# The delta rule's mixer: shifted sums from TensorE to ScalarE and VectorE, TensorE left with the turns

## The reference

```python
def fractal_mixer(x, conv_w):
    out = 2.0 * x
    for i in range(conv_w.shape[0]):            # 4 taps
        dil = 2 ** i                            # back by 1, 2, 4, 8 tokens
        x_shift = jnp.pad(x, ((0, 0), (dil, 0), (0, 0)))[:, :l, :]
        out = out + x_shift * conv_w[i, :, 0] + x * conv_w[i, :, 1]
    return out

frac = rmsnorm(fractal_mixer(x, frac_conv_w), mixer_norm_w)
gate = sigmoid(x @ frac_gate_w + frac_gate_b)
return core + gate * frac                       # core: the delta rule itself
```

## Time and profile before

| | before |
|---|---|
| median of 3 runs | 2610.37 us (2606.3 to 2613.95) |
| the profiled execution: time, span | 2605.69 us, 2603.9 us |
| PE busy | 2413.8 us (93%) |
| DVE busy | 1696.0 us (65%) |
| ACT busy | 1216.3 us (47%) |
| POOL busy | 1334.0 us (51%) |
| mean granted TensorE clock | 0.976 of full speed |

### The profile page before, as it was taken

How to read it: one execution, slowest core, us unless ns; L and a number is a source line. 1 busy time by engine, 2 the same in 40 slices (tenths; PEclk the granted TensorE clock), 3 DMA queues, 4 the chain that set the end, 5 groups by cost and what they waited for, 6 DMA issues and landing times. The chain is left out here.

```text
span 2603.9 us, 56605 instructions
## 1 busy us (share of the span) xinstructions
PE 2413.8 (93%) x20854; PEld 2007.2 (77%) x20854; DVE 1696.0 (65%) x4060; ACT 1216.3 (47%) x3095; POOL 1334.0 (51%) x1465
## 2 busy tenths in 40 slices
PE   4899999999999999878999999988899999999998
PEld 3788888888888888756777877756677778778776
DVE  4576777767677767576767767326756746747664
ACT  2656666666666666455444445114333333332332
POOL 3676776767676767256555555214522323322322
PEclk8999999999999999989999999988999999999999
DMA  4000100000000000012112111206112112212211
GB/s 141 7 10 9 45 17 11 9 10 10 10 10 9 9 5 5 15 31 45 42 47 49 36 53 43 55 31 187 33 52 68 62 42 74 66 42 62 64 39 58
DMA packets 156688, 105.05 MB, mean 40 GB/s; under 512 B 85168, under 2 KB 134832, under 8 KB 156416
## 3 DMA queue, kind: packets, MB, share of 16 engines
q1 hardware_dynamic: 131072, 62.83, 8.9%
q10 hardware_dynamic: 25344, 38.60, 4.8%
HBM read 80.51 MB, written 20.88 MB: 39 GB/s over the span
## 5 line engine op out<-in xcount | busy, mean ns | idle before, releaser
L920 POOL TENSOR_TENSOR a_bm<-a_bias,a_mask_add 128x512 f32<-128x512 f32 (+3 forms) x512 | 437.8, 871 | 191.0 <-DVE a_nm L674 186.0
L1529 POOL TENSOR_TENSOR m_hid_part<-m_hid,m_hid_part 128x512 fp32r<-128x512 f32 x176 | 239.5, 1361 | 564.1 <-ACT m_hid_part L1438 561.0
L830 ACT ACTIVATE a_S<-a_S,a_nm 128x512 f32<-128x512 f32 (+3 forms) x512 | 289.2, 565 | 346.4 <-DVE a_nm L674 343.6
L674 DVE CUSTOM_DVE_ANT_0 a_S<-a_S,a_bm,a_nsn 128x512 f32<-128x512 f32 (+3 forms) x512 | 275.4, 545 | 141.2 <-PE a_S L438 136.9
L461 PE MATMUL a_O<-a_v,a_PT 128*128 128x64 f32 x2560 | 342.4, 265 | 0.0
L461 PEld LDWEIGHTS a_O<-a_v,a_PT 128*128 128x128 f32 x2560 | 328.4, 193 | 0.0
L1450 ACT ACTIVATE m_hid<-m_G 128x512 f32<-128x512 f32 x176 | 105.4, 599 | 408.4 <-PE m_G L1384 371.3
L438 PE MATMUL a_S<-a_kT,a_qT 128*128 128x384 f32 (+3 forms) x1024 | 284.3, 359 | 3.5 <-DVE a_nm L674 3.0
L1401 PE MATMUL m_Y<-m_hid_part,m_down_high 128*128 128x512 f32 x704 | 257.3, 406 | 11.9 <-POOL m_hid_part L1529 11.1
L1611 DVE TENSOR_TENSOR m_hid<-m_hid,m_U 128x512 f32<-128x512 f32 x176 | 121.0, 687 | 223.6 <-PE m_U L1384 189.7
L1384 PE MATMUL m_G<-m_in,m_gate_high 128*128 128x512 f32 x704 | 251.5, 398 | 1.6 <-POOL m_up_low L1523 1.6
(11 more groups left out here) (314 smaller groups left out, 5240.2 us busy)
## 6 DMA issues: line engine op xcount, KB each, us to landing
m_spread<-s_w ACTq DMA_DIRECT2D x64, 256.0 KB, 3.3
m_spread<-s_w ACTq DMA_DIRECT2D x128, 128.0 KB, 2.9
a_x<-in_x SPq DMA_DIRECT2D x32, 128.0 KB, 2.1
s_hT<-a_hT SPq DMA_DIRECT2D x32, 128.0 KB, 2.1
d_x<-in_x SPq DMA_DIRECT2D x8, 512.0 KB, 4.8
d_h<-s_hT SPq DMA_DIRECT2D x8, 512.0 KB, 5.4
s_xg<-d_xg SPq DMA_DIRECT2D x8, 512.0 KB, 3.1
d_x<-s_xg SPq DMA_DIRECT2D x8, 512.0 KB, 4.5
```

What stands on the lines that cost most here:

```text
L674: dve.tensor_tensor_reduce(S[:, n % S_SLOTS, 0:w], SB[n % 2][:, 0:w], bm[:, n % BM_SLOTS, 0:w], -1.0, nsn[:, tile % 2, h:h + 1], ALU.add, ...
L830: act.activation(S[:, n % S_SLOTS, 0:w], S[:, n % S_SLOTS, 0:w], ACT.Exp, scale=-1.0, bias=nm[:, tile % 2, h:h + 1], accum_out=den[:, tile ...
L920: pool.tensor_tensor(bm[:, n % BM_SLOTS, 0:w], bias[:, h, L - w:L], mask_add[b % 2][:, 0:w], ALU.add).then_inc(s["bm_ready"], 1)
L1529: pool.tensor_tensor(hid_part[1][:, q % H_SLOTS], hid[:, q % G_SLOTS], hid_part[0][:, q % H_SLOTS].bitcast(F32), ALU.subtract).then_inc(hi ...
```

## The change

The sums move off PE. In the round of the batch itself (lag IN) ACT makes the first term for each channel half, 128x512 from `h` by `own` (`tap` 0 and 1), and DVE adds the four shifted terms in place with four chained STT of 128x512 (`mix` 0 and 1). The result `mx` takes the place of the `diag` matrices in SBUF. One round later (lag F) PE turns the sums: two transposes per `mixer` piece in place of 20 passes. `frac`, `fve`, `frs` and `xg` follow with lag F as well. There is one `mx`, so the taps of a batch wait until mixer 3 of the batch before has been turned, in the same round. SP's load of the next `h` waits for `mix`, the projections and the gates where it waited for the mixer, and SP sends `xg` one round later. In the preamble ten small DVE products that built `diag` go.

```diff
-        diag = sb("diag", [P, KD, 5, P])
+        mx = sb("mx", [P, KD, L])
@@ PE_ROUND
-            ("step", 1, R), ("fast", 1, R), ("M", 2, R), ("mixer", 0, IN), ("M", 3, R),
+            ("step", 1, R), ("fast", 1, R), ("M", 2, R), ("mixer", 0, F), ("M", 3, R),
...
(mixer 1, 2, 3: the same, IN becomes F)
@@ ACT_ROUND (frac 0 to 3: IN becomes F)
-            ("frac", 2, IN), ("qkT", 1, IN), ("uw", 1, F),
+            ("frac", 2, F), ("qkT", 1, IN), ("uw", 1, F), ("tap", 0, IN),
             ("qkT", 2, IN), ("uw", 2, F), ("silu", 5, IN),
-            ("frac", 3, IN), ("uw", 3, F), ("qkT", 3, IN),
+            ("tap", 1, IN), ("frac", 3, F), ("uw", 3, F), ("qkT", 3, IN),
@@ DVE_ROUND (xg 0 to 3: IN becomes F)
-            ("S", 10, R), ("x1", 1, K),
-            ("S", 11, R), ("fve", 0, IN), ("attn", 1, F), ("low", 0, IN),
+            ("S", 10, R), ("x1", 1, K), ("mix", 0, IN),
+            ("S", 11, R), ("fve", 0, F), ("attn", 1, F), ("low", 0, IN), ("mix", 1, IN),
@@ SP
-                            sp.wait_ge(mixer_psum, TT * bi)
+                            sp.wait_ge(mix_ready, KD * bi)
+                            sp.wait_ge(proj_psum, 6 * bi)
+                            sp.wait_ge(gates_psum, bi)
...
-                    if bi < B:
-                        sp.wait_ge(xg_ready, TT * (bi + 1))
+                    if 0 <= bf < B:
+                        sp.wait_ge(xg_ready, TT * (bf + 1))
@@ PE
                     elif name == "mixer":
+                        pe.wait_ge(mix_ready, KD * (b + 1))
                         o = fill(name, i, b)
                         for k in range(KD):
-                            at = PAD + i * P
-                            for j in range(5):
-                                back = 0 if j == 4 else 2 ** j
-                                last = pe.matmul(o[:, k * P:(k + 1) * P],
-                                                 h[b % 2][:, k, at - back:at - back + P], diag[:, k, j],
-                                                 start=j == 0, stop=j == 4)
+                            last = pe.transpose(o[:, k * P:(k + 1) * P], mx[:, k, i * P:(i + 1) * P], ident[:])
@@ ACT
+                    elif name == "tap":
...
+                            act.wait_ge(h_in[b % 2], 16 * ((b + 1) // 2))
+                            act.wait_ge(mixer_psum, TT * b)
+                        act.activation(mx[:, i], h[b % 2][:, i, PAD:], ACT.Copy, scale=own[:, i:i + 1]).then_inc(mix_tap, 1)
@@ DVE, preamble
-                for k in range(KD):
-                    for i in range(5):
-                        w = own[:, k:k + 1] if i == 4 else frac[:, k, i, 0:1]
-                        dve.tensor_scalar(diag[:, k, i], ident[:], w, None, ALU.mult)
@@ DVE
+                    elif name == "mix":
+                        dve.wait_ge(mix_tap, KD * b + i + 1)
+                        for j in range(4):
+                            at = PAD - 2 ** j
+                            ins = dve.scalar_tensor_tensor(out=mx[:, i], in0=h[b % 2][:, i, at:at + L],
+                                                           scalar=frac[:, i, j, 0:1], in1=mx[:, i],
+                                                           op0=ALU.mult, op1=ALU.add)
+                            if j < 3:
+                                link(ins)
+                        ins.then_inc(mix_ready, 1)
```

More of the change, by code:

```diff
@@ L1761, in delta_phase @@
         nb_ready = sem("nb_ready")
+        own_ready = sem("own_ready")
+        mix_tap = sem("mix_tap")
+        mix_ready = sem("mix_ready")
         mixer_psum = sem("mixer_psum")
@@ L1830, in delta_phase @@
             ("step", 4, R), ("fast", 4, R), ("qp", 1, R), ("z", 2, IN), ("Z", 0, F),
-            ("step", 5, R), ("fast", 5, R), ("hold", 0, K), ("hold", 1, K), ("hold", 2, K), ("hold", 3, K), ("onT", 0, K), ("onT", 1, K), ("z", 3, IN), ("mixer", 1, IN),
+            ("step", 5, R), ("fast", 5, R), ("hold", 0, K), ("hold", 1, K), ("hold", 2, K), ("hold", 3, K), ("onT", 0, K), ("onT", 1, K), ("z", 3, IN), ("mixer", 1, F),
             ("step", 6, R), ("fast", 6, R), ("TZ", 0, F), ("core", 0, K), ("au", 3, R),
             ("step", 7, R), ("fast", 7, R), ("qkT", 0, IN), ("uw", 0, F), ("attn", 0, F),
-            ("step", 8, R), ("fast", 8, R), ("mixer", 2, IN), ("qkT", 1, IN), ("uw", 1, F),
+            ("step", 8, R), ("fast", 8, R), ("mixer", 2, F), ("qkT", 1, IN), ("uw", 1, F),
             ("step", 9, R), ("fast", 9, R), ("core", 1, K), ("qkT", 2, IN), ("uw", 2, F),
-            ("step", 10, R), ("fast", 10, R), ("mixer", 3, IN), ("uw", 3, F), ("qkT", 3, IN),
+            ("step", 10, R), ("fast", 10, R), ("mixer", 3, F), ("uw", 3, F), ("qkT", 3, IN),
             ("step", 11, R), ("fast", 11, R), ("attn", 1, F), ("gram", 0, IN), ("attn", 2, F), ("gram", 1, IN),
@@ L1843, in delta_phase @@
             ("ocopy", 0, K), ("ocopy", 1, K), ("M", 1, R), ("silu", 0, IN), ("silu", 1, IN), ("proj", 4, IN),
-            ("M", 2, R), ("osq", 0, K), ("silu", 2, IN), ("M", 3, R), ("frac", 0, IN),
+            ("M", 2, R), ("osq", 0, K), ("silu", 2, IN), ("M", 3, R), ("frac", 0, F),
             ("M", 0, R), ("silu", 3, IN), ("z", 0, IN),
@@ L1866, in delta_phase @@
             ("S", 9, R), ("qk", 3, IN), ("conv", 5, IN),
-            ("S", 10, R), ("x1", 1, K),
-            ("S", 11, R), ("fve", 0, IN), ("attn", 1, F), ("low", 0, IN),
-            ("S", 12, R), ("attn", 2, F), ("low", 1, IN), ("attn", 3, F), ("xg", 0, IN),
-            ("S", 13, R), ("vb", 0, IN), ("conv", 0, NX), ("xg", 1, IN),
-            ("S", 14, R), ("vb", 1, IN), ("conv", 1, NX), ("xg", 2, IN), ("gates", 0, NX), ("xg", 3, IN)]
+            ("S", 10, R), ("x1", 1, K), ("mix", 0, IN),
+            ("S", 11, R), ("fve", 0, F), ("attn", 1, F), ("low", 0, IN), ("mix", 1, IN),
+            ("S", 12, R), ("attn", 2, F), ("low", 1, IN), ("attn", 3, F), ("xg", 0, F),
+            ("S", 13, R), ("vb", 0, IN), ("conv", 0, NX), ("xg", 1, F),
+            ("S", 14, R), ("vb", 1, IN), ("conv", 1, NX), ("xg", 2, F), ("gates", 0, NX), ("xg", 3, F)]
         POOL_ROUND = [
             ("kb", 0, F), ("gxm", 0, F), ("ors", 0, K), ("nb", 0, IN), ("rot", 0, IN), ("rot", 1, IN), ("rrn", 0, IN),
-            ("rot", 2, IN), ("rrn", 1, IN), ("rot", 3, IN), ("rrn", 2, IN), ("rrn", 3, IN), ("frs", 0, IN),
+            ("rot", 2, IN), ("rrn", 1, IN), ("rot", 3, IN), ("rrn", 2, IN), ("rrn", 3, IN), ("frs", 0, F),
             ("off", 0, IN), ("inv", 0, IN), ("inv", 1, IN)]
@@ L2194, in _ @@
                                        scale=conv[:, i // 2, i % 2, 0:1]).then_inc(tap_ready, 1)
+                    elif name == "tap":
+                        if b == 0:
+                            act.wait_ge(own_ready, 1)
+                            act.wait_ge(delta["h0_in"], 16)
+                        else:
+                            act.wait_ge(h_in[b % 2], 16 * ((b + 1) // 2))
+                            act.wait_ge(mixer_psum, TT * b)
+                        act.activation(mx[:, i], h[b % 2][:, i, PAD:], ACT.Copy, scale=own[:, i:i + 1]).then_inc(mix_tap, 1)
                     elif name == "silu":
```

12 lines of the change are left out of this document (5 added, 7 removed).

## The result

The changed kernel takes 2624.0 us in the median (2618.2 to 2636.5), the kernel before beside it 2608.2; the ratio is 1.0066, 95% interval [1.0044, 1.0087]. In a second comparison it was 1.0056 [1.0028, 1.0084]. So it is slower by about 0.6%, some 16 us. The profiled execution took 2618.2 us with a span of 2616.4 (before 2605.7 and 2603.9). The mean granted clock over the whole span is 0.948, before 0.976.

What follows compares the result with a forecast made beforehand. A steady round was taken to be as long as TensorE's work. The terms, -21.4 + 4.3 + 1.0 + 10.1 = -6.0 us, took the median from 2610.4 to 2604.4 us, range 2591 to 2619.

Steps and rivals of the forecast that it cites:

- (d): Rival: steady rounds don't shorten because VectorE loses its small gaps; +5 to +12 us, 2615.7 to 2622.4; chance 0.13.
- the clock's term: Between au 0 and au 1, small tiles drop PE to 1.2 GHz once in each of six rounds, 2.85 us each: +10.1.
- PE's saving, the bound and the order: PE bounds steady rounds; turned mixers free 8.6 us of it; mixes hide; PE idles some 2.4 us before gram 0.
- The steady round at full clock, -3.85 us: Walk through round 1427: -4.0 us by step 12, 0.15 given back by low 1's later end.
- mixer 0: Behind step 1: ScalarE's idle time before z 0 limits the gain to -1.4 us at step 3.
- mixer 1: Behind step 5: VectorE's dense chain absorbs PE's 2.1 us; running gain -1.0, then -1.65 us at qk 1.
- mixer 2: Behind step 8: 2.05 us of hidden time comes free, running gain -3.7 us at qkT 1 and steps 9 and 10.
- mixer 3 with the taps: Before gram 0: taps hold ScalarE's queue, 5.9 us against 6.2; only 0.3 of 2.1 left, running gain -4.0 at step 12.
- rival (b): A second clock fall each round before gram 0, about 2.5 us a round, 15 in all: +9, 2619.4 us; chance 0.15.
- Rounds without steps, +4.3: In the two start rounds mixes aren't hidden and delay low 1, the inversion and Z: first step 4.3 us later.
- Round 1640, +1.0: Last round with F work: no proj, four turned mixers on PE, while Z waits 3.8 us anyway: +1.0 us.
- The two falls of before: Clock falls in rounds 1498 and 1573 of the kernel before, 3.5 us each, subtracted from the six forecast falls.

Runs made afterwards that it cites:

- e5: Changed kernel plus two unread bf16 128x512 products behind every recurrence step, 32 a round: 2617.6 us, 1.0014 of the kernel before.
- e6: Kernel before plus two unread bf16 128x512 products behind every recurrence step, 32 a round: 2641.8 us, 1.0105 of the kernel before.
- The pair with fillers: e5 and e6, the changed kernel and the kernel before with the same unread products behind every step: 2617.6 and 2641.8 us.
- e14: Changed kernel plus second `mx` tile and unread products at the start rounds' waits, behind steps 0 to 2 and every step of batch 5's round: 2596.2 us, 0.9942.
- e13: Kernel before plus unread products in the start rounds and two behind each of steps 0, 1 and 2: 1.0021 of the kernel before.
- e15: Kernel before plus exactly the unread products of e14, without the change or second tile: 1.0046 of the kernel before.
- e3: Kernel before, its mixers still on PE, plus the change's taps and mixes with their sums never read: 2627.7 us, 1.007.
- e8: Changed kernel with two `mx` tiles used in turn, so taps don't wait for mixer 3; no fillers: 2609.0 us, 0.9983 of the kernel before.

## Why the prediction was wrong

I forecast 2604.4 us, range 2591 to 2619. The time, 2624.0, was above the range, and the kernel got slower and not faster. The nearest rival by number is (d), 2615.7 to 2622.4, but its mechanism, VectorE's small gaps, is not what happened: e5 and e6 rule it out. The step that failed is the clock's term. Point by point:

- **PE's saving, the bound and the order** were right: 7.8 us of PE a round (8.6 put), hidden mixes, S 11 and S 12 in place, PE released at gram 0 by the copy of qkT. Its size there was not: 0.8 us in place of 2.4. The walk's own terms (5.9 us, against 6.2 less 2.1) give only 1.8; and gram 0 came 5.0 us after mixer 3 and not 5.9, since the pieces on ScalarE started 0.6 us apart behind a tap and 0.5 behind the others, where I had put 0.72 and 0.66.
- **The steady round at full clock, -3.85 us**: too small, not too large. The pair with fillers gives -6.4; e14, with the second tile, has 66.8 us where before with the same 1.3 us of fillers (e13, e15) has 72.8 to 73.7. By the table of steps, mixer 0 was worth 2.06 us (1.4 put), mixer 1 0.7 (0.25 put), mixer 2 2.0 (2.05 put) and mixer 3 with the taps 1.7 (0.3 put); the last is the largest miss, the queue of the point above. VectorE's chain from S 4 to S 8 kept its length, as I had said. No run has the changed kernel without fillers at full clock. An estimate for it: its steady rounds less half of their time at the lower clock are 64.5 to 64.9 us, 6 under 71.0, if all of PE's loss lengthens the round.
- **The clock, one fall a round, 2.85 us**: this step failed. The place of the first fall was right (in each of the six rounds, 9 to 10 us in). But there are two or three, 10.2 to 17.1 us at the lower level in each steady round. Half of that is lost to PE, 5.1 to 8.5 us, and a steady round gains 0.7 on average, where at full clock, by the pair with fillers, it gains 6.4. A second fall was rival (b), and that fall exists, 54 to 57 us in, in two of the four rounds. The more frequent one I had not seen: 33 to 38 us in, in all four, in three of them at qkT 1 and uw 1, right behind 0.6 us in which PE waits for qk 1, and with PE busy for 3.30 of 3.30 us inside.
- **Rounds without steps, +4.3**: measured +9.7. e3, with the mixes and PE's old load, has +2.3, e8 +4.2. The rest, 5.5, goes with the 17.1 us at the lower clock right before the first step (3.4 in e8), with PE busy in all of it. I had written a clock term for the rounds and none for the start.
- **Round 1640, +1.0**: measured +7.5, +8.5 in the second execution. The long fall; no row of before showed one, and I bounded the clock's cost by falls of 6.8 us.
- **The two falls of before**: I took them as what before has. It had four the second time, and the median of before already carries some of that.

In one sentence: the relief was larger than I said, the clock took most of it in the steady rounds, and it took more at the start and in the round of batch 6, where there was nothing to gain. An estimate of the clock's share: with equal fillers one `mx` stands 0.35% under before (1.0011 against 1.0046; 0.9% by e5 and e6), without them 0.66% over it. That 1.0%, 26 us (1.6%, 41 us, by e5 and e6), is what the clock's behaviour turned; it is somewhat too high, since in the changed kernel a part of the fillers falls into PE's idle time, 2.1 to 2.6 us a steady round; the 0.7 to 0.8% of the tap's wait comes on top, and a part of that is again the clock.

The Trainium skill, in "TensorE: Matmul & The Clock Gate", Part 1, section "HAM oscillation — how this bites in real kernels", explains such losses by gaps in which PE is idle between its pieces. The long stretch above does not agree: 40.60 us at 1.2 GHz with PE busy for 40.60, as far as the profile, which models the ends of matmuls, can tell. The same part's statement that the throttled clock is the default and activity releases it does agree with e5, where added products kept the clock up and brought the time down. It is not the whole of it: five pairs of the same products stand inside the long stretch, behind the first steps of its round, and didn't bring the clock back at once.

**What stays open**: why the same products fall in one round and not in the next; where fillers belong to hold the clock at the least cost (with few of them falls only moved about); how long a steady round of the changed kernel is at full clock without fillers; and the 6 us of "everything else".

## What to carry to other kernels

Where a kernel is bound by PE and runs at full clock, price the removal of dense products at both clock levels: count what is left between the dense pieces, in every stretch, the start and the tail included, and look in more than one trace of the old kernel for falls (that one fall means that the rest is near one is my guess from two kernels). If the clock then falls, a few unread products behind the small-tile pieces can be cheaper than the falls, but they must be measured against the old kernel with the same fillers. And a buffer whose reader is late holds its writer's whole queue: a second tile was worth 0.7 to 0.8% here, and the moved work, with the same fillers on both sides, 0.35 to 0.9%.

## What the hardware showed that I had not expected

- A stretch of 41 to 44 us at 1.2 GHz in which the profile shows PE never idle, repeated in a second execution, and not seen where two unread products stood behind every step of the round in front. Two such products behind each step inside it did not end it for 28 us.
- The same PE work, to 0.01 us, with a fall in one round and none in another, and two against four falls in two executions of one kernel.
- 32 unread products of 128x512 in bf16 cost 7.0 us of a full PE, 0.22 us each; in the changed kernel 32 a round made the program 0.5% faster.
